# A Mamba block in front of a switch FFN: where VectorE's work and the small steps of the main loop stand

## What is computed

```python
h = concat(cls, patches @ W.T + b)                      # [64, 197, 192]
x = layernorm(h)                                        # no gamma
xz = x @ W_in; x_inner, z = split(xz)                   # 384 each
x_conv = silu(conv1d(x_inner, conv_w) + conv_b)         # 4 taps over tokens, 384 -> 384
B, C = split(x_conv @ W_x)                              # 16 states each
delta = softplus(x_conv @ W_dt + b_dt)
# scan over the tokens, for each of 384 channels and 16 states
h_s = exp(delta * A) * h_s + (delta * x_conv) * B
y = sum_s(h_s * C) + D * x_conv
out = (y * silu(z)) @ W_out
h = h + layernorm(out) * gamma + beta
h = h + switch_ffn(layernorm(h))                        # argmax route, rank in its expert,
                                                        # at most CAP tokens per expert
```

## Time and profile before

| | us |
|---|---|
| median of 3 runs | 3121.68 (3120.38 to 3123.74) |
| the profiled execution | 3125.05 |
| its span, first to last instruction | 3123.3 |
| PE busy | 2551.4 (82%) |
| VectorE busy | 2516.7 (81%) |
| GpSimd busy | 2153.0 (69%) |
| ScalarE busy | 1970.8 (63%) |

### The profile page before, as it was taken

How to read it: one execution, slowest core, us unless ns; L and a number is a source line. 1 busy time by engine, 2 the same in 40 slices (tenths; PEclk the granted TensorE clock), 3 DMA queues, 4 the chain that set the end, 5 groups by cost and what they waited for, 6 DMA issues and landing times.

```text
span 3123.3 us, 38093 instructions
## 1 busy us (share of the span) xinstructions
PE 2551.4 (82%) x12714; PEld 1570.2 (50%) x12714; DVE 2516.7 (81%) x2800; ACT 1970.8 (63%) x3883; POOL 2153.0 (69%) x1291
## 2 busy tenths in 40 slices
PE   5688888878888888888888878788886567999997
PEld 3344444444444444444444444444442256888886
DVE  1499999999999999999999999999999875322222
ACT  0577777777777777777777777777676464333332
POOL 0378788877888887778888887788787613544442
PEclk8899899988899999989999998888898679999999
DMA  3344444444554544444444444454453023666652
GB/s 95 93 94 101 102 101 105 115 115 108 114 118 116 115 107 102 102 102 101 102 101 101 102 117 106 114 114 114 108 118 91 8 74 111 220 215 206 210 188 99
DMA packets 165466, 361.10 MB, mean 116 GB/s; under 512 B 18353, under 2 KB 89593, under 8 KB 157848
## 3 DMA queue, kind: packets, MB, share of 16 engines
q1 hardware_dynamic: 152504, 329.59, 42.0%
q0 software_dynamic: 12768, 29.08, 2.9%
HBM read 293.86 MB, written 69.30 MB: 116 GB/s over the span
## 4 chain that ended last, share of the span: by engine, by line
PE 38%; DVE 33%; issue 13%; ACT 13%; POOL 1%; DMA 1%; SPq 0%; DVEq 0%; POOLq 0%; ACTq 0%
DVE arena L1311 15%; DVE arena L1302 11%; PE banks L1218 7%; PE banks L1197 5%; PE banks L941 4%; PE banks L904 4%; PE banks L1205 2%; PE banks L970 2%; PE banks L932 2%; PE banks L923 2%; ACT banks L661 2%; ACT arena L668 1%; DVE arena L1340 1%; DVE arena L1285 1%; ACT L741 1%
## 5 line engine op out<-in xcount | busy, mean ns | idle before, releaser
L489 POOL TENSOR_TENSOR arena<-arena 128x1576 f32<-128x1576 f32 x384 | 1244.2, 3255 | 286.7 <-DVE arena L1311 286.7
L1311 DVE TENSOR_TENSOR_SCAN arena<-banks,arena 128x788 f32<-128x788 f32 x768 | 1359.8, 1789 | 58.7 <-ACT banks L661 20.5
L661 ACT ACTIVATE banks<-arena,neg_a 128x392 f32<-128x392 f32 x1536 | 842.3, 581 | 421.8 <-DVE arena L1311 415.2
L1302 DVE TENSOR_TENSOR arena<-arena,banks 128x1576 f32<-128x1576 f32 x384 | 681.3, 1774 | 29.4 <-DMA arena<-delta_du_scratch 16.8
L970 PE MATMUL banks<-arena,gather_q 128*32 128x394 f32 x3072 | 380.2, 571 | 0.2 <-POOL arena L489 0.2
L1513 DVE TENSOR_TENSOR arena<-banks,arena 128x384 f32<-128x384 f32 x57 | 31.8, 558 | 346.3 <-PE banks L1218 346.3
L904 PE MATMUL banks<-wtok,arena 128*99 128x192 f32 x1536 | 264.3, 329 | 49.1 <-ACT arena L728 44.3
L923 PE MATMUL banks<-arena,v_lo 128*128 128x394 f32 x768 | 291.5, 523 | 2.5 <-ACT arena L698 1.1
L904 PEld LDWEIGHTS banks<-wtok,arena 128*99 128x99 f32 x1536 | 249.0, 167 | 81.2 <-ACT arena L728 65.6
L624 POOL DMA_INDIRECT out_tokens<-arena x114 | 114.7, 1006 | 245.0 <-DVE arena L1528 225.2
L668 ACT ACTIVATE arena<-arena 99x192 f32<-99x192 f32 x384 | 178.8, 536 | 124.2 <-POOL arena L483 119.6
(11 more groups left out here) (217 smaller groups left out, 4237.8 us busy)
## 6 DMA issues: line engine op xcount, KB each, us to landing
arena<-delta_du_scratch SPq DMA_DIRECT2D x384, 394.0 KB, 11.2
arena<-in_w_pack SPq DMA_DIRECT2D x57, 1155.0 KB, 5.2
delta_du_scratch<-arena SPq DMA_DIRECT2D x96, 394.0 KB, 3.3
arena<-in_x SPq DMA_DIRECT2D x32, 1176.0 KB, 15.8
rows_scratch<-arena SPq DMA_DIRECT2D x32, 297.0 KB
rows_scratch<-arena SPq DMA_DIRECT2D x32, 294.0 KB
arena<-in_b SPq DMA_DIRECT2D x57, 96.0 KB, 5.2
arena<-in_conv_w SPq DMA_DIRECT2D x1, 2304.0 KB, 9.1
```

What stands on the lines that cost most here:

```text
L489: pool.tensor_tensor(v[:, :, :], v[:, :, :], c_rep[r][:, u % NG].unsqueeze(1).to_broadcast([P, NQ, N2]), ALU.mult).then_inc(s_mulp, 1)
L661: ins = act.activation(o, d, ACT.Exp, scale=neg_a[:, c:c + 1])
L1302: dve.tensor_tensor(hb[u % BUFS][:, :, :], rep[m][:, :, 1, :], ps_b[:, 0:N2].unsqueeze(1).to_broadcast([P, NQ, N2]), ALU.mult).then_inc(s_ ...
L1311: dve.tensor_tensor_scan(v, decay[k % 2], v, 0.0, ALU.mult, ALU.add).then_inc(s_scan, 1)
```

## The change

Of the twelve products with B of a pair, those of units 5 and 9 are made by GpSimd (bx_pool) instead of VectorE. GpSimd can't read PSUM, so ScalarE keeps a copy of the spread B (keep_b, taken at unit 1, which has the same group of states as units 5 and 9). The ring of hb has five buffers in place of six, counted through over the pairs.

Small steps leave VectorE: the last subtraction of B and C goes to GpSimd with a rounding copy on ScalarE (last_bc, third_bc); the (e + 1) - 1 of softplus becomes two ScalarE passes (softplus_up, softplus_t); the statistics of the output product become a sum of squares on ScalarE (out_squares) and one small step on GpSimd (rstd_out). For that the output weights are centred once (w_sum), so that the output's mean is zero.

All steps are placed anew. The convolution is made one pair earlier (conv(i + 2) at the end of body i); row statistics, row norm, back transposes, router and logits of a pair come one body later (i - 2 in place of i - 1). choose(FIRST), rank(FIRST) and ranks(FIRST) now stand behind the loop, shift(FIRST) in body 32 and weigh(FIRST) in body 33, each after that body's take_logits. SyncE's body is unchanged.

The diff, cut to its core:

```diff
-BUFS = 6
+KEEP = 1
+BY_POOL = (5, 9)
+BXS = UNITS - len(BY_POOL)
+BUFS = 5
...
+            def rstd_out(n):
+                need(pool, s_onorm, n)
+                pool.wait_ge(s_sq2, n + 1)
+                pool.tensor_scalar(var2[:, :], sq2[:, :], 1.0 / DIM, EPS, ALU.mult, ALU.add).then_inc(s_var2, 1)
+                pool.wait_ge(s_var2, n + 1)
+                pool.tensor_tensor(rs2[:, :], var2[:, :], small[0:H0, 0, :], ALU.pow).then_inc(s_rs2, 1)
...
+            def bx_pool(n, u):
+                pool.wait_ge(s_rep[u // NG], REP * (n + 1))
+                pool.wait_ge(s_bkeep, n + 1)
+                need(pool, s_ysum, UNITS * n + u - BUFS + 1)
+                pool.tensor_tensor(hb[(UNITS * n + u) % BUFS][:, :, :], rep[u // NG][:, :, 1, :], b_keep.unsqueeze(1).to_broadcast([P, NQ, N2]),
+                                   ALU.mult).then_inc(s_bxp, 1)
...
+            def last_bc(n, r):
+                pool.wait_ge(s_bcmid, n + 1)
+                pool.tensor_tensor(bcf, bcf, bc3[r], ALU.subtract).then_inc(s_bclast, 1)
...
+            def out_squares(n, r):
...
+                for c in range(4):
+                    ins = act.activation(rows[r][:, c, DIM:2 * DIM], ob[:, c, :], ACT.Square, accum_out=sq2[:, c:c + 1])
+                ins.then_inc(s_sq2, 1)
...
+            def keep_b(n):
+                act.wait_ge(s_bx, bx_count(n, KEEP) + 1)
+                need(act, s_bxp, len(BY_POOL) * n)
+                act.activation(b_keep, ps_b[:, 0:N2], ACT.Copy).then_inc(s_bkeep, 1)
...
+            def third_bc(n, r):
+                act.wait_ge(s_bclast, n + 1)
+                act.activation(bc3[r][P - 2 * NS:P], bcf[P - 2 * NS:P], ACT.Copy).then_inc(s_bc3, 1)
...
+            def softplus_up(n):
+                act.wait_ge(s_spe, n + 1)
+                need(act, s_ddu, DDU * n)
+                act.activation(delta[:, :, :], spe[:, :, :], ACT.Identity, bias=1.0).then_inc(s_spu, 1)
+
+            def softplus_t(n):
+                act.wait_ge(s_spu, n + 1)
+                act.activation(delta[:, :, :], delta[:, :, :], ACT.Identity, bias=-1.0).then_inc(s_spt, 1)
```

More of the change, by code:

```diff
@@ L292, in build @@
         s_bx = sem("bx_ready")
+        s_bxp = sem("bx_by_gpsimd_ready")
+        s_bkeep = sem("b_kept")
         s_scan = sem("scan_done")
@@ new lines, in body @@
+                    if 1 in on and k == 1:
+                        silu_x(i + 1, o)
+                    if 0 in on and k == 2:
+                        keep_b(i)
+                    if -2 in on and k == 3:
+                        row_norm(i - 2, r)
+                        if i == PAIRS + 1:
+                            router_exp(FIRST, 1)
+                    if 1 in on and k == 3:
+                        copy_product(i + 1, o, r, BC)
+                    if 1 in on and k == 4:
+                        copy_product(i + 1, o, r, DT + 2)
@@ L1015, in body @@
                 for u in range(UNITS):
-                    if 0 in on and u + 1 < UNITS:
+                    if 0 in on and u + 1 < UNITS and u + 1 not in BY_POOL:
                         spread_b(i, r, u + 1)
@@ new lines, in body @@
+                    if -1 in on and u == 2:
+                        if 1 in on:
+                            pe.wait_ge(s_gev, 10 * (i + 1) + 6)
+                        else:
+                            pe.wait_ge(s_lg, i - 3 + 1)
+                        out_product(i - 1, r, 0)
+                    if 0 in on and u == 3:
+                        if 1 in on:
+                            pe.wait_ge(s_gev, 10 * (i + 1) + 7)
+                        else:
+                            pe.wait_ge(s_cc, NG * i + 3)
+                        spread_c(i, r, r, 3)
@@ L1025, in body @@
+                    if 2 in on and u == 3:
+                        if -1 in on:
+                            pe.wait_ge(s_oev, 2 * (i - 1) + 1)
+                        elif 1 in on:
+                            pe.wait_ge(s_gev, 10 * (i + 1) + 6)
+                        tok(i + 2, r, 0)
+                    if 2 in on and u == 3:
                         if 0 in on:
                             pe.wait_ge(s_cc, NG * i + 4)
-                        else:
-                            pe.wait_ge(s_h, 2 * (i + 1) + 2)
@@ L1048, in body @@
+                    if -1 in on and u == 5:
+                        if 2 in on:
+                            pe.wait_ge(s_h, 2 * (i + 2) + 2)
                         elif 0 in on:
@@ L1103, in body @@
+                    if 2 in on and u == 7:
                         if 1 in on:
@@ L1143, in _ @@
                 body(i, i % 2, range(-i, PAIRS - i))
+            rank(FIRST, 1)
             rank(LAST, 2)
@@ L1438, in _ @@
                 body(i, i % 2, range(-i, PAIRS - i))
+            choose(FIRST)
+            ranks(FIRST, 1)
             shift(LAST)
```

433 lines of the change are left out of this document (218 added, 215 removed).

## The result

The changed kernel takes 2972.55 us (median of 4 runs, 2970.36 to 2982.04), the kernel before in the same session 3122.71: ratio 0.953, 95% interval 0.9515 to 0.9544. The forecast was 2945, with a range of 2895 to 3055. The profiled execution took 2973.0 us; its span is 2971.3.

What follows compares the result with a forecast made beforehand. GpSimd at 66.9 us a pair was to bound, just above VectorE's 65.2; with 0.4 of waits 67.3 against 73.55, 200 us saved in 32 pairs, 23 lost behind the loop: 2948 profiled, 2945 median, range 2895 to 3055.

Steps and rivals of the forecast that it cites:

- VectorE, 65.2 a pair: VectorE's own chain in the loop: 73.55 less 7.33 of work and holes of 0.57 and 0.47 us, giving 65.2.
- GpSimd, 66.9 a pair: GpSimd's loop load: 59.84 plus 6.44 for two products, plus 0.93, less 0.35, making it the bound at 66.9 us.
- The small waits: Waits in the loop that neither VectorE nor GpSimd can hide: 0.4 us a pair added to GpSimd's 66.9, giving 67.3.
- more small waits: Rival, 17%: ScalarE has three or four places with a decay late by a microsecond, paid by VectorE: 68.8 a pair, 2993 us.
- Where the two meet: VectorE's scans of units 5 and 9, at T = 28 and 50; GpSimd's products arrive about T = 27 to 30 and 50 to 52.
- The ring of five: Five buffers in place of six cost nothing, since product u already had to wait for the sum of u - 5.
- Behind the loop: After the loop, choice, sums and ranks of all images but the last two now come one behind the other: +23 us.
- The prologue: Before the first embedding, centring the output weights costs VectorE 1.6 us under the load it waits for: 0, at most 2.
- The squares and their sums: ScalarE in the loop: four summed squares, read-outs adding 0 to 0.8 us; four table loads stay four if squares need none.
- The late patches: Rival, 14%: the patch load takes its old 15.8 us and holds VectorE's embeddings some 4 us: 70.5 a pair, 3047 us.
- the lock: Rival, 1%: GpSimd and VectorE block each other, each new product holding off a scan: 73.8 us a pair, 3153 us.
- the slow chain: Rival, 5%: TensorE's three convolution products at the pair's end run at the lower clock, 6.7 us late: 73.3 a pair, 3137 us.

Runs made afterwards that it cites:

- three moves and unit 5's product alone: Changed kernel with patches issued early, softplus and C steps later, routing early, and unit 9's product back on VectorE: 0.9339 of the kernel before, 67.18 us a pair.
- The experiment that moved the steps: Changed kernel with two softplus passes moved behind decay 8, copy of C and third part of B and C behind decay 9: 0.9488, 67.62 us a pair.
- Routing early: Changed kernel with routes of all images but the last four worked out during the last pair's chain: 0.9435 of the kernel before, 68.18 us a pair.
- the patches early: Changed kernel with SyncE issuing the patches of pair i + 3 ahead of its wait for the rows of pair i - 1: 0.9443, 67.41 us a pair.

## Why the prediction was right, and where it was off

**VectorE, 65.2 a pair: right.** The table gives 65.2 and the kernel with three moves and unit 5's product alone 65.25. Busy time is 64.1 (64 was named as the sign). One line was read wrongly on the way. The hole of 0.47 before the scan at 1080.16 isn't a decay waiting for its delta: that scan's decay had ended at 1077.86, before the product in front of the scan began.

```profile
1076.77 1.09 ACT L661 ACTIVATE banks<-arena,neg_a 128x392 f32<-128x392 f32 x2
```

The view names the product before it as what ended the hole, and such a hole comes 3 times between 500 and 2200 us. The sum holds in spite of it, because VectorE's waits in the kernel before are 1.1 us a pair on average (25.5 us in 23 pairs), as much as the two holes together.

**GpSimd, 66.9 a pair: too high as a sum, wrong as the bound.** Its busy time is 65.3 (1632.70 us by 25 pairs), 1.6 less and below the 66.5 to 67.9 that were given. The product was 2.99 and not 3.22, 0.46 less for two, and below even the 3.04 of the nearest row. The pair of the earlier trace rows had 59.84 of busy time where the mean of 23 pairs was 59.5; what else makes the 1.6 was not broken down. The step that failed is the next one: "GpSimd becomes the bound, by a hair". It set GpSimd's 66.9 against a VectorE of 65.2, or of 65.8 to 66.7 with two late decays. VectorE has 3.1 us of waits in its chain, which makes it 68.3 in the middle of the loop, and GpSimd waits for it 2.3 us a pair. Added work of 1.47 on GpSimd cost 0.12.

So there is luck in the number. The sum went by an engine that didn't bind, and that engine's term was 1.6 too high, which made up for waits of VectorE that had not been counted.

**The small waits: the mis-sized term.** The sum allowed 0.4 above GpSimd, that is 2.1 above VectorE's 65.2; they are 3.1. One by one:

- Decay 8 was taken as 0.3 late and is 1.36. The bunch itself fits: 7.0 us (1032.70 to the end of the first half pair, 1039.73) against 6.8. But decay 7 starts at 1031.68, behind a bias step at 1031.20 (the second of two), and not when its bank is free, 1030.9 (where the two scans before end). That 0.8 had been left out. The experiment that moved the steps removed the wait.
- The second embedding was given 0 to 1 and lost 0.9, but it wasn't in the sum, being thought hidden under GpSimd. The load's 11.9 us lies in the 9 to 12 named, TensorE's wait of 2.2 on average (3.3 at most) just above the 0 to 2. That the products behind this wait run at a lower clock, 9.4 us in place of 8.0, wasn't in the prediction at all.
- Decay 18 was given 0.3 to 1.2 and costs 0.23.
- Scan 2 was given a slack of 0.7 and loses 0.45 on average: nothing in 13 of 25 pairs, 1.55 in the five in which TensorE's clock fell just before (last section), 0.2 to 0.6 in seven.

That is the mechanism of the rival "more small waits", which put 68.8 a pair and 2993 us. The measured 68.06 lies midway between it and the forecast's 67.3, and 2972.55 at the upper end of the forecast's own band (2913 to 2974).

**Where the two meet: in time, but the sign named for it didn't show.** VectorE was to be idle before the scans of units 5 and 9. Of products made on GpSimd it waited for none: scan 10 starts 1.69 us after scan 9 in every pair, and what scan 18 waits for is its decay. The products of GpSimd end 1.8 and at least 2.2 us before these scans start. The ring of five shows no wait of its own among VectorE's; GpSimd's wait of 2.1 us in 1700 for a state sum (L521 behind L1054) is all of it.

**Something was missed that didn't show in the number.** The prediction priced the two products at 3.74 us of VectorE. They are worth 6.1, since unit 5's also frees VectorE from the pick that stands behind the patch products. I had laid TensorE's order out for the state sums and the convolutions and not for the picks, because with the product on GpSimd this pick isn't there. The forecast was safe only since it dealt with the change as a whole, which is luck again.

**Behind the loop: right.** +23 was said and +21.5 measured; the rank scan is 22.0 later. Routing early gave it back (0.953 to 0.9435), so it was a matter of order and not of work.

**The prologue: small miss.** 0 to 2 was said and +4.0 seen in the profiled execution; the experiments' kernels, which share most of it, began their first scan between 125.2 and 128.4 us. What the 4 are made of was not tested.

**The squares and their sums: right.** Each read-out takes 0.19 us (four a pair, 0.8, the upper end given), and the table loads stayed four a pair: 98 in 25 pairs. ScalarE's busy time ended at 57.2 us a pair and not at about 59, and TensorE's 60.03 us at 0.92 would be 55.2 at the full clock, not some 56; neither decided anything.

```profile
L731 ACT ACTIVATION_READ_ACCUMULATOR arena<-arena 99x1 f32 x100 | 19.0, 190 | 0.0
```

In numbers, from 2945 to 2972.55: the loop gave 22.5 less (177.5 of 200), the first scan is 4.0 later against the 0 taken, and the end 1.5 better, together 25.0. Another 2.95 comes from the profiled execution lying 0.45 above its median and not 3.4, and 0.35 goes in rounding.

The late patches, the lock and the slow chain as full rivals fell. The patches took 11.9 us and not 15.8. The scans last 1786 ns on average beside a GpSimd that is busy 96% of the time, as against 1789 on average before (the page, part 5): no hold.

## What to carry to other kernels

When an engine is relieved until another one comes level, compare the second engine's load with the first one's chain including its waits, decay by decay and not with an allowance. With two engines within 2 us of each other the waits of the first one decide which of them binds. Look for moves in sets: taking away the wait of scan 8 (1.36 us) gave 0.44 us a pair alone, since the next wait on the same engine grew, and with the patches early the two gave 1.6. And before a product is called worth its duration, look at what its other operand stands behind in the queue of the engine that makes it.

## What the hardware showed unexpectedly

GpSimd's time for one shape hangs on its operands. 128x1576 takes 3.26 us with C (L514) and 2.99 as the product with B (L521), within 0.01 us of this in all kernels that were run. What in the operands makes it (broadcast, number of tiles) was not tested.

TensorE's clock falls in the middle of a loop in which the engine is busy for 86% of the time: of the 1700 us it stood at the lower level for 133. It costs in two places. One is the patch products, behind TensorE's wait for the load: 9.4 us in place of 8.0, in nearly every pair. The kernel with the patches early has neither the wait nor the fall. The other is behind the take of y. In both stretches below TensorE had been idle 1.92 us for the take of y. In the first it went on at a mean granted clock of 0.79, in the second at 1.00.

```profile
1010.34:1018.50 8.16, 8.16 (x31) 3.21 (x31) 7.95 (x9) 5.82 (x10) 7.33 (x3) 0.79 0.00 0
1079.41:1087.00 7.59, 6.86 (x31) 2.88 (x31) 7.49 (x7) 6.84 (x10) 7.59 (x3) 1.00 0.01 3
```

```profile
1010.34 1.54 PE L1050 MATMUL banks<-arena,skip 128*128 128x394 f32 x2 [1.92 <-DVE arena L1426]
1011.81 1.54 PE L1054 MATMUL banks<-arena,gather_q 128*32 128x394 f32 x8
...
1079.41 0.93 PE L1050 MATMUL banks<-arena,skip 128*128 128x394 f32 x2 [1.92 <-DVE arena L1426]
1080.27 0.87 PE L1054 MATMUL banks<-arena,gather_q 128*32 128x394 f32 x8
```

The state sum and the skip product took 3.0 us and not 1.7, the convolution behind them ended 1.6 us later, and scan 2 of that pair came 6.62 us after scan 1, of the other 5.07. It is the "slow convolution chain" in small, in five of 25 pairs, 0.31 us a pair on average. Five of the other pairs in which scan 2 is late, by 0.6, follow a pair whose scan 22 was late, by 0.4 to 1.2, with the clock at its lower level there.
